# Four graph layers on 64 graphs: joint scores of layers 0 and 2, a mask moved to VectorE, loops unrolled, new order tables

## The reference

```python
def layer0(x, adj):                       # 8 heads of 32, 4 hops
    q, k, v = x @ Wq.T + bq, x @ Wk.T + bk, x @ Wv.T + bv
    p = softmax(where(adj == 0, -16384, heads(q) @ heads(k).T))
    z = heads(v)
    for _ in range(4): z = 0.9 * (p @ z) + 0.1 * heads(v)
    return layernorm(x + z) * gamma + beta
def layer1(x, adj):                       # one head of 256
    w = softmax(where(adj == 0, -inf, (x @ Wq) @ (x @ Wk).T / 16))
    return layernorm(x + (w @ (x @ Wv)) @ Wo + bo) * gamma + beta
def layer2(x, adj):                       # 8 heads of 32, one hop
    p = softmax(where(adj == 0, -inf, heads(q) @ heads(k).T / sqrt(32)))
    return layernorm(x + (p @ heads(v)) @ Wo + bo) * gamma + beta
def layer3(x, adj):                       # 4 edge labels, then a gated unit
    w_d = (adj == d) / (count + 1e-8)     # d = 1..4
    out = relu(concat(w_d.T @ x) @ Wd.T + bd)
    r, z = sigmoid(out @ Wri.T + x @ Wrh.T + b), sigmoid(out @ Wzi.T + x @ Wzh.T + b)
    n = tanh(out @ Wni.T + bni + r * (x @ Wnh.T + bnh))
    return layernorm((1 - z) * n + z * x) * gamma + beta
```

## Time and profile before

| | |
|---|---|
| median of 3 runs | 1782.2 us (1782.07 to 1782.91) |
| the profiled execution | 1783.61 us |
| its span, first to last instruction | 1781.8 us |
| TensorE busy | 1728.4 us, 97% |
| ScalarE, VectorE, GpSimd busy | 67%, 62%, 45% |
| granted TensorE clock, mean | 0.987 of full |
| DMA, mean | 28 GB/s |

### The profile page before, as it was taken

The page is one execution under the profiler, slowest core; times in us unless marked ns, Lnnn a source line. Parts: engine busy times, 40 slices in busy tenths (PEclk is TensorE's granted clock), DMA queues, the critical chain, the costliest instruction groups (busy, mean ns, idle before and its releaser), DMA issues.

```text
span 1781.8 us, 48249 instructions
## 1 busy us (share of the span) xinstructions
PE 1728.4 (97%) x17680; PEld 1549.8 (87%) x17680; DVE 1102.2 (62%) x2741; ACT 1190.9 (67%) x4008; POOL 793.9 (45%) x774
## 2 busy tenths in 40 slices
PE   5799999999999999999999999999999999999995
PEld 4688899998899998899998899998899998889885
DVE  3665666665666665666665666665666666666662
ACT  4576777666777666776666776666777666677652
POOL 1354444444444444444444544444544454544441
PEclk8999999999999999999999999999999999999998
DMA  5000011000000000001001011000011000000000
GB/s 182 27 22 25 20 31 31 17 27 29 18 29 29 20 22 29 18 29 29 23 18 29 18 29 29 27 14 29 18 29 29 29 12 29 19 28 21 13 16 13
DMA packets 70982, 49.39 MB, mean 28 GB/s; under 512 B 4368, under 2 KB 69904, under 8 KB 70288
## 3 DMA queue, kind: packets, MB, share of 16 engines
q1 hardware_dynamic: 70928, 48.66, 9.1%
HBM read 40.26 MB, written 8.39 MB: 27 GB/s over the span
## 4 chain that ended last, share of the span: by engine, by line
PE 93%; issue 2%; DVE 2%; ACT 2%; POOL 1%; DMA 0%; SPq 0%; POOLq 0%; DVEq 0%
PE bank_A L375 15%; PE bank_B L375 10%; PE bank_A L409 7%; PE bank_A L602 6%; PE bank_A L424 5%; PE bank_B L593 5%; PE bank_A L593 5%; PE bank_B L424 4%; PE bank_C L418 3%; PE bank_X L387 3%; PE bank_X L375 3%; PE bank_C L375 3%; PE bank_B L387 2%; PE bank_X L520 2%; PE bank_A L563 2%
## 5 line engine op out<-in xcount | busy, mean ns | idle before, releaser
L802 POOL TENSOR_TENSOR E<-E,rsum 128x512 f32<-128x512 f32 x256 | 266.4, 1041 | 565.3 <-DVE rsum L898 420.2
L810 POOL TENSOR_TENSOR rstd<-var,minus_half 128x2 f32<-128x2 f32 x128 | 92.4, 722 | 283.2 <-DVE var L933 277.4
L409 PEld LDWEIGHTS bank_A<-kT,qT 32*128 32x128 f32 x1024 | 123.2, 186 | 36.4 <-issue 27.1
L680 ACT ACTIVATE vnat<-bank_A 128x256 f32<-128x256 f32 x96 | 36.9, 384 | 170.0 <-PE bank_A L486 169.9
L375 PE MATMUL bank_A<-xT_hi,w_hi 128*128 128x256 f32 x512 | 138.8, 294 | 11.6 <-DVE xT_lo L869 11.6
L409 PE MATMUL bank_A<-kT,qT 32*128 32x128 f32 x1024 | 147.6, 283 | 0.5 <-ACT E L669 0.5
L409 PE MATMUL bank_B<-kT,qT 32*128 32x128 f32 x1024 | 147.6, 283 | 0.0
L375 PE MATMUL bank_A<-xT_hi,w_lo 128*128 128x256 f32 x512 | 132.3, 281 | 0.0
L834 POOL TENSOR_TENSOR E<-E,rcnt 128x512 f32<-128x512 f32 x64 | 78.3, 1245 | 113.7 <-DVE rcnt L1005 113.7
L693 ACT ACTIVATE xT_hi<-bank_A,col 128x256 fp32r<-128x256 f32 x128 | 65.3, 562 | 94.5 <-PE bank_A L393 94.5
L409 PEld LDWEIGHTS bank_B<-kT,qT 32*128 32x128 f32 x1024 | 123.2, 186 | 0.0
(11 more groups left out here) (198 smaller groups left out, 6143.9 us busy)
## 6 DMA issues: line engine op xcount, KB each, us to landing
adj<-in_adj SPq DMA_DIRECT2D x96, 128.0 KB, 2.4
xt_in<-in_xt SPq DMA_DIRECT2D x64, 128.0 KB, 2.2
x_in<-in_x SPq DMA_DIRECT2D x32, 256.0 KB, 2.7
out<-out_sb SPq DMA_DIRECT2D x32, 256.0 KB, 2.2
absent<-in_adj SPq DMA_DIRECT2D x32, 128.0 KB, 2.1
stage<-in_weights SPq DMA_DIRECT2D x3, 1024.0 KB, 10.7
row<-in_rows SPq DMA_DIRECT2D x1, 1152.0 KB, 10.1
stage<-in_l_weights SPq DMA_DIRECT2D x1, 1024.0 KB, 7.5
```

Of the source, the lines that this page charges most:

```text
L409: mm = nc.tensor.matmul(b[:, at:at + P], qT[hs, c, ns], kT[hs, c, ns], start=masked_by is None, stop=masked_by is None or (g, c) == (G - 1 ...
L802: nc.gpsimd.tensor_tensor(e, e, rs[:, part].unsqueeze(2).to_broadcast([P, SB, P]), ALU.mult).then_inc(e_sig.sem, 1)
L810: nc.gpsimd.tensor_tensor(rstd[part][:], var[part][:], minus_half[:], ALU.pow)\
```

## The change

Four things, made together.

1. Steps `s0` and `s2` become one step `s02` on TensorE. Its part 0 does heads 0 and 1 (partitions 0 to 63) of layer 0 for round n and heads 2 and 3 (partitions 64 to 127) of layer 2 for round n - 2 (`APART`), in turn, into four banks; part 1 the other pairs. It waits for both layers' operands, and for the exponentials of both before part 1. At the ends only one of the layers has a round, and `s02` runs for 34 periods (`EXTRA`).
2. Layer 2's mask is no longer a product on TensorE: VectorE's `fill2` writes it over the scores, as `fill0` does; GpSimd's `ne2` becomes `absent.2`.
3. The loop is gone: all periods are written out. The counters `dve_passed` and `pool_passed`, incremented after three kinds of wait, go with it. Two small additions (`eps`, `guard`) become reductions over a pair with a stored constant.
4. All order tables are new. `store` now lags 8 periods, layer 3 on TensorE lags 4.

```diff
-def periods(eng, engine):
+APART = 2
+EXTRA = {"s02": APART}
+HEADS2 = [2, 3, 0, 1]
+def periods(engine):
     steps = table(engine)
-    for n in [*range(LAST_LAG + 1), None, *range(ROUNDS, ROUNDS + LAST_LAG)]:
-        if n is None:
-            with eng.Fori(LAST_LAG + 1, ROUNDS) as now:
...
+    for n in range(ROUNDS + LAST_LAG):
+        for step, part, lag in steps:
+            if 0 <= n - lag < ROUNDS + EXTRA.get(step, 0):
+                yield step, part, n - lag
...
     "tensor": [
-        "hop2.1@2 ri@3 hop0.6 hop0.7 wo2.0@2 back0.6 wo2.1@2 n2@1 back0.7",
+        "hop0.5 p2.3@2 wt.0@3 back0.4 back0.5 hop2.0@2 hop0.6",
...
-            def scores(banks, qT, kT, pair, masked_by=None):
-                if masked_by is not None:
-                    for b in banks:
-                        nc.tensor.matmul(b[:, :], ident_b[:], masked_by[:].unsqueeze(2).to_broadcast([P, G, NC, P]),
-                                         start=True, stop=False)
+            def scores(runs):
                 for g in range(G):
                     for c in range(NC):
                         at, ns = (g * NC + c) * P, slice(g * P, (g + 1) * P)
-                        for j, b in enumerate(banks):
+                        for banks, qT, kT, heads in runs:
+                            for b, h in zip(banks, heads):
+                                hs = slice(h * HD, (h + 1) * HD)
+                                mm = nc.tensor.matmul(b[:, at:at + P], qT[hs, c, ns], kT[hs, c, ns],
+                                                      start=True, stop=True)
...
+                if step == "s02":
+                    runs, ready = [], []
+                    if exists(it):
+                        if part == 0:
+                            wait(pe, k0_ready, it, 1)
+                            wait(pe, q0_ready, it, 1)
+                        else:
+                            wait(pe, exp0, it, 2)
+                        runs.append((AB0, qT0, kT0, (2 * part, 2 * part + 1)))
+                    it2 = it - APART
+                    if exists(it2):
+                        if part == 0:
+                            wait(pe, q2_ready, it2, 1)
+                            wait(pe, v2_ready, it2, 1)
+                        else:
+                            wait(pe, exp2, it2, 2)
+                        runs.append((AB2, qT2, kT2, HEADS2[2 * part:2 * part + 2]))
+                    scores(runs).then_inc(s02_ready.sem, 1)
...
-                if step == "fill0":
+                if step in ("fill0", "fill2"):
...
-                        pause(dve, s0_ready, it, part // 2 + 1, dve_passed)
+                        wait(dve, s02_ready, it + APART if L == 2 else it, part // 2 + 1)
...
+                    nc.vector.copy_predicated(s, m, f).then_inc((filled0 if L == 0 else filled2).sem, 1)
```

More of the change, by code:

```diff
@@ L88, in table, with exists @@
     return steps
-LAST_LAG = max(lag for engine in ORDER for _, _, lag in table(engine))
-def periods(eng, engine):
-    steps = table(engine)
-    for n in [*range(LAST_LAG + 1), None, *range(ROUNDS, ROUNDS + LAST_LAG)]:
-        if n is None:
-            with eng.Fori(LAST_LAG + 1, ROUNDS) as now:
[L100 to L105, removed]
+APART = 2
+EXTRA = {"s02": APART}
+HEADS2 = [2, 3, 0, 1]
+LAST_LAG = max(lag + EXTRA.get(step, 0) for engine in ORDER for step, _, lag in table(engine))
+def periods(engine):
+    steps = table(engine)
+    for n in range(ROUNDS + LAST_LAG):
+        for step, part, lag in steps:
+            if 0 <= n - lag < ROUNDS + EXTRA.get(step, 0):
+                yield step, part, n - lag
+def exists(it):
+    return 0 <= it < ROUNDS
 def starts(it):
-    return isinstance(it, int) and it == 0
+    return it == 0
 class Signal:
@@ L160, in gnn_program @@
         row = sb("row", [P, len(ROWS), D])
-        fill = sb("fill", [P, 1])
+        fill0, fill2 = sb("fill0", [P, 1]), sb("fill2", [P, 1])
         minus_half = sb("minus_half", [P, G])
@@ L209, in gnn_program @@
         stats = [sb(f"stats{L}", [P, G, 6]) for L in range(4)]
-        mv = [sb(f"mv{L}", [P, G, 2]) for L in range(4)]
+        mv = [sb(f"mv{L}", [P, G, 3]) for L in range(4)]
         var = [sb(f"var{L}", [P, G]) for L in range(4)]
@@ L237, in gnn_program @@
         v0_back, vn0_ready = signal("v0_back", 1), signal("vn0_ready", 1)
-        s0_ready, filled0, max0, exp0, r0_ready, e0_ready, p0_t, pt0_ready = (
-            signal(n, k) for n, k in (("s0_ready", 2), ("filled0", 4), ("max0", 4), ("exp0", 4), ("r0_ready", 4),
+        s02_ready = signal("s02_ready", 2)
+        filled0, max0, exp0, r0_ready, e0_ready, p0_t, pt0_ready = (
+            signal(n, k) for n, k in (("filled0", 4), ("max0", 4), ("exp0", 4), ("r0_ready", 4),
                                       ("e0_ready", 4), ("p0_t", 4), ("pt0_ready", 4)))
@@ L340, in _ @@
             load_weights(3)
-            sp.wait_ge(w_split, SPLIT["2"])
-            load_weights(4)
-            for step, part, it in periods(sp, "sync"):
+            for step, part, it in periods("sync"):
                 if step == "ld_xt" and not starts(it):
@@ L351, in _ @@
                 if step == "ld_adj" and not starts(it):
-                    if part == 0:
-                        wait_before(sp, filled0, it, 4)
-                    elif part < 3:
-                        wait_before(sp, (None, ne1_ready, ne2_ready)[part], it, 1)
+                    if part in (0, 2):
+                        wait_before(sp, filled0 if part == 0 else filled2, it, HC)
                     else:
-                        wait_before(sp, masked, it, 1)
+                        wait_before(sp, ne1_ready if part == 1 else masked, it, 1)
                     load_adj(part, it)
+                if step == "ldw" and starts(it):
+                    sp.wait_ge(w_split, SPLIT["2"])
+                    load_weights(4)
                 if step == "store":
@@ L419, in transpose_heads, with attend @@
                 return mm
-            def attend(bank, vnat, PT, g):
+            def attend(bank, vnat, PT, g, order=range(HC)):
                 for h in range(HEADS):
@@ L429, in _ @@
             pe.wait_ge(cols_made, 1)
-            for step, part, it in periods(pe, "tensor"):
+            for step, part, it in periods("tensor"):
                 if step == "k0":
@@ L460, in _ @@
                     mm.then_inc(v0_back.sem, 1)
-                if step == "s0":
-                    if part == 0:
-                        wait(pe, k0_ready, it, 1)
-                        wait(pe, q0_ready, it, 1)
-                    else:
-                        wait(pe, exp0, it, 2)
-                    scores(AB0, qT0, kT0, part).then_inc(s0_ready.sem, 1)
+                if step == "s02":
[16 more added lines that the diff above has]
+                    scores(runs).then_inc(s02_ready.sem, 1)
                 if step == "p0":
@@ L541, in _ @@
                     natural(B2, "v2", xT_hi[2], xT_lo[2]).then_inc(proj2.sem, 1)
-                if step == "s2":
-                    if part == 0:
-                        wait(pe, q2_ready, it, 1)
-                        wait(pe, v2_ready, it, 1)
-                        wait(pe, ne2_ready, it, 1)
-                    else:
-                        wait(pe, exp2, it, 2)
-                    scores(AB2, qT2, kT2, part, no_edge2).then_inc(s2_ready.sem, 1)
                 if step == "p2":
@@ L638, in _ @@
             act.wait_ge(cols_made, 1)
-            for step, part, it in periods(act, "scalar"):
+            for step, part, it in periods("scalar"):
                 if step == "x0":
@@ L850, in split_lo @@
                                         group(w_hi, j).bitcast(F32), ALU.subtract).then_inc(w_split, 1)
-            nc.vector.memset(fill[:], -16384.0)
+            nc.vector.memset(fill0[:], -16384.0)
+            nc.vector.memset(fill2[:], -3e38)
             nc.vector.memset(minus_half[:], -0.5)
+            for t in mv:
+                nc.vector.memset(t[:, :, 2], LN_EPS)
+            nc.vector.memset(cnt[:, :, :, 1], DEG_EPS)
             dve.wait_ge(col_loaded, 16)
@@ L864, in _ @@
             split_lo(0)
-            for step, part, it in periods(dve, "vector"):
+            for step, part, it in periods("vector"):
                 if step == "x0":
```

82 lines of the change are left out of this document (34 added, 48 removed), and 26 rows, old and new, of the table ORDER.

## The result

The changed kernel takes 1689.5 us (median of four runs, 1688.9 to 1690.3) where the kernel before takes 1782.1: a ratio of 0.948, 95% interval 0.947 to 0.949, or 93 us less. The forecast was 1671, its own range 1655 to 1690, the range 1653 to 1715. So the direction and the mechanism came out, the time lies at the upper edge of the forecast's own range, and 18 us of the gain are missing.

A forecast was written before the change was run, and what follows sets the result against it. TensorE's instructions were taken to bound full periods: savings of 2.48, 0.86 and 0.6 us cut 53.29 to 49.35; 159.1 + 28 x 49.35 + 130.4 = 1671.3 us of span, forecast 1671 us, own range 1655 to 1690, range 1653 to 1715.

The forecast's parts named there:

- What bounds it: Full periods: nothing but TensorE's own instructions sets the time, with one wait of 0.6 us from 165 to 1700 us.
- Joint scores: TensorE's score steps: two joint steps take 2.48 us with their changes where four took 4.96, 2.48 us less a period.
- The forecast's lower bound: Joint score steps: nothing gained but the two changes of layout, 0.68 us a period.
- The rival with pairs only: Joint score steps: the array takes two row groups at once, not four; 1724 us, chance 0.10.
- the price that I set beside it: Joint score step at the skill page's speedup of 3.07: 1.15 us, the time some 16 us longer.
- The mask: Layer 2's scores lose TensorE's mask products, 0.86 us less a period; VectorE's four copies cost nothing if not waited for.
- Hops: TensorE's layout changes: 0.31 us for each group of hops, six groups become four, 0.6 us less a period.
- The margin at the second half: Joint step's second half: exponentials ready after 9.1 us against 9.8 of TensorE's work, no wait, 0.7 us to spare.
- Fill: Start of the kernel: period 4 starts its projection at 159.1 us, 15 us earlier.
- stay as they are: Periods 0 and 1 in the fill: layer 0's chain, unchanged at 69.9 us.
- Drain: End of the kernel, after the 28 full periods: 130.4 us, 14.8 more, as layer 3 costs one period more.

The follow-up runs named there:

- a_same_rows: The changed kernel with layer 2's heads in the joint step in the same 64 partitions as layer 0's, so two row groups instead of four: 1742.7 us.
- b_mask: The kernel before, periods written out, with layer 2's mask moved from TensorE to VectorE copies in the old order: 1811.7 us.
- b_mask_sp: The kernel before, written out, layer 2's mask on VectorE, and layer 1's adjacency load ahead of layer 2's on SyncE: 1784.6 us.
- b_mask_act: The kernel before, written out, layer 2's mask on VectorE, layer 1's load ahead of layer 2's, ScalarE's vo1 ahead of exp2.0: 1770.1 us.
- a_fill_twice: The changed kernel with every masking copy of layers 0 and 2 done twice on VectorE, with a semaphore between: 1790.4 us.
- b_unroll: The kernel before with every period written out instead of looped, nothing else changed: 1782.0 us.
- a_split_late: The changed kernel with the splitting of weight group 1 put back beside split.2, on ScalarE and VectorE: 1690.7 us.
- a_layer_by_layer: The changed kernel with all of layer 0's products in the joint step issued ahead of layer 2's, four row groups kept: 1723.4 us.
- a_fill1: The changed kernel with layer 1's mask also moved from TensorE's two products to a VectorE copy: 1680.3 us.

## Why the prediction was right, and where its sizes were off

From the kernel before to the changed one, the periods of the table make a ladder: 53.29, mask on VectorE 52.74, hops together 52.14, joint steps of the same rows with the rest of the new order 51.23, four row groups 49.47.

- **What bounds it.** TensorE's own instructions, before and after; one wait of 0.6 us in the full periods of the first, none in the second. Right.
- **Joint scores.** Forecast 2.48 us a period: 1.76 for the four row groups and 0.72 for the changes of layout of two steps saved. Measured 1.76 (a_same_rows against the changed kernel) and 0.91, the latter with the rest of the new order in it, which no run takes apart. (The forecast's lower bound has 0.68 for the two changes, from 0.19 and 0.15, where its sum has 0.72; neither decides anything.) The rival with pairs only, 1724, was wrong. So was the price that I set beside it from the Trainium skill, "TensorE: Matmul & The Clock Gate", section "Measured speedup vs the span model": its 3.07 for four row tiles, taken as a rate, would have made the 32 records 1.15 us and the time 16 us longer. The timeline has them in 0.88, a full four (0.11 us for each four), with no loss against the pairs' two. The trace decides, for the rate inside a step. The page's number is for products of 512 columns, where ours have 128; whether it includes a beginning and an end, as our 1.11 us does, the page doesn't say.
- **The mask.** Forecast 0.86, costed at nothing on VectorE. In the old order it is worth less than nothing (b_mask, 30 us slower), then nothing (b_mask_sp), then 0.55 (b_mask_act). The step "I cost it at nothing as long as it is not waited for" failed in the old order, where the copies were waited for. In the new tables TensorE has no wait, but no run measures the mask there by itself. The rest of the 0.86 appears, if at all, in the ladder's next rungs: all terms together are 3.82 against 3.94 forecast, and that 0.12 a period, **3.4 us** in all, is the miss in the full periods.
- **Hops.** Forecast 0.31 for a group of hops less; half of 0.61 and of 0.60 measured. Right.
- **The margin at the second half.** Forecast: exponentials done 9.1 us after the first half, second half due after 9.8. In the trace the next step after the first half begins at 1020.77, ScalarE's last exponential starts at 1029.51 and what follows it at 1029.85, and the second half begins at 1030.65. That is 9.1 and 9.9. Its parts came out too, so it was not luck: VectorE's ninth instruction ends 6.1 us after the first half (6.2 forecast), and ScalarE's first exponential starts after 3.6 (3.5); that so small a margin is enough in every period, and no more than enough, is what a_fill_twice shows.

```profile
1029.51 0.46 ACT L727 ACTIVATE E<-bank_B,nmax 128x128 f32<-128x128 f32 x1
...
1029.85 0.70 ACT L656 ACTIVATE vnat<-bank_C 128x512 f32<-128x512 f32 x1
```
```profile
1030.65 0.37 PE L403 MATMUL bank_A<-kT,qT 32*128 32x128 f32 x1
```

- **Fill.** The step that failed: `k0` of period 4 was forecast at 159.1 and came at 169.4, **10.3 us** late, most of the miss. Periods 0 and 1, which were to "stay as they are", took 73.1, not 69.9. Period 0 did stay (37.5 us, 37.6 before), and the 3.2 us are period 1's, where the forecast left the granted clock out: with the same work TensorE ran at 0.81 of full speed, against 0.92 before. The length of this period goes with the clock across the kernels: 31.1 us at 0.97 (b_unroll), 31.6 at 0.95 (a_split_late), 34.1 at 0.90 (a_layer_by_layer), 35.6 at 0.81 here, 36.1 at 0.76 (a_fill1). Why it was lower in some is open, and no run sets it. Period 2 was put at 37, between 35.8 and 39.7, and took 39.8. Period 3 was put at 40.7 and took 44.9, 7.9 of them idle. Since layer 3 now comes a period later, there is nothing to stand between the two halves of a softmax in periods 2 and 3, and a saving on TensorE there only lengthens a wait. TensorE's waits from 124.46 to 169.37 us:

```profile
PE bank_X L373 <- DVE xT_lo L944: 3.7, 1, 3.7
PE bank_C L411 <- POOL E L795: 1.8, 2, 1.5
```

  The first is layer 1's normalised input, the second layer 0's probabilities: chains of the other engines, which the change does not shorten. That is read from the waits, for periods 2 and 3; no experiment tests it, and a_split_late only excludes the place of the split.
- **Drain.** Forecast 130.4; from 169.37 and 28 periods of 49.47 to the span's end it is 133.0, **2.6 us** more.

10.3 + 3.4 + 2.6 = 16.3 us of span. The rest of the 18 is the median, which I had put 1.4 below the profiled run and which equals it here, and 0.7 by which I had rounded the sum down to 1671.

## What to carry to other kernels

Where TensorE works on products of 32 rows, put as many row groups as there are side by side, from different layers if need be, and issue them in turn and not one layer after the other. When work moves off the bounding engine, walk through the queues of all the others for what stands behind the new wait (here one DMA, then one copy): the same edit was worth +30, +3 and -12 us by the place of two words. Forecast fill and drain from the chains of latency there and from the granted clock, not from the savings of the full periods.

## What the runs showed of the hardware

- Four row groups take four 32x128 by 128 fp32 products every 0.11 us, the same spacing as a pair, or as one full product of 128 rows.
- TensorE starts products of a free row group past waiting ones, but not past many: in a_layer_by_layer layer 2's first starts at layer 0's fifth pair of eight, which makes a step 0.33 us shorter than with two row groups (1.65 against 1.98) and 0.54 longer than with the layers in turn. Which records are whose is inferred from their lengths.
- In the fill, where TensorE waits, its granted clock differs from kernel to kernel: period 1, 278 to 281 TensorE records, took 31.1 us at 0.97 of full speed and 36.1 at 0.76, while the full periods have 1.00.
- An engine with idle time can still be without spare: doubling eight copies on VectorE, 67% busy, cost TensorE 3.15 us a period.
- Writing the loop out costs and gives nothing (1782.0 against 1782.6), though the instruction queue moves four times the bytes: `q8 instruction` has 140 packets and 2.29 MB in the changed kernel, 35 and 0.57 MB before (141 and 2.31 MB in b_unroll).
